# Cross-attention and a routed FFN on one core: another order of the attention's steps on four engines, and identity transposes in TensorE's waits

## The chip, the cores and the metric

The kernel runs on one core of a Trainium2 chip. Time is device time of one launch in microseconds (us). The kernel before took 2058.97 us, the median of three runs (2055.81 to 2060.05).

## The reference

Inputs: x (16 sequences of 224 tokens, 512 wide), a context (16 x 750 x 384) and a mask over the context. All arithmetic is in fp32.

```python
x = x + xattn(layernorm(x), ctx, mask, Wq, Wk, Wv, Wo, bo)    # 8 heads of 64, softmax over 750 keys
x = x + ffn(layernorm(x), Wr, W1, W2)                         # 8 experts, top 2, at most 1120 tokens each
# ffn: probs = softmax(xf @ Wr); for each expert e the tokens that chose it:
#      y[idx] += gate * (relu(xe @ W1[e]) @ W2[e])            # W1 512x2048, W2 2048x512
```

In the given inputs the unmasked keys that matter (see below) lie in the last 192 of the 750.

## The kernel before

**Arithmetic.** TensorE gets each fp32 operand as a high part and a low part (the remainder), and a product is three matrix products: high by high, high by low, low by high. ScalarE writes the high part while it copies a result out of PSUM, VectorE subtracts to get the low part. So a product that feeds another one is followed by a step on ScalarE and one on VectorE.

**Preamble** (`preamble`, L69). Identity, constants, a flag from the mask. Where every sequence has its masked-in keys only in the last 192 positions, the short attention runs (`attention_short`, L281), which is the case here.

**Attention.** The 16 sequences go in 8 pairs p. Each of a pair's steps has a kind and a number, and each engine executes its own steps in an order that is written out by hand in a string; a step waits on semaphores for what it needs, and everything behind it on its engine waits with it. On TensorE the kinds are:

- fc0-2, fx0-3: transposes of the context and of the normalized x of the *next* pair (written ahead for it); k0-3, q0-3, v0-3: projections; k0 and q0 too are those of the next pair.
- s0-15: scores of one head and sequence (16 units per pair), 192 keys. VectorE adds the mask and takes the maximum, ScalarE the exponential and its sum (2 instructions each), GpSimd the reciprocal and the scaling (u). Then t0-15: transposes of the probabilities (ScalarE and VectorE split them), then o0-15: the product with v (two heads share a result; the odd one ends it).
- A negative number (t-3, o-4) is a unit of the pair before: t13 to t15 and o12 to o15 of a pair are done in the pass after it. So are wo0-3 (output projection, residual, statistics of the second layernorm), tt0-3 (transposes of its result), lg0 (router logits) and lt0 (their transposes).

The kinds q, k, v, fx, fc, wo, tt, lg (`RINGED`) take turns in two PSUM banks psJ, in TensorE's order: each waits until the one two before it has been split or copied (`proj`, L731: `pe.wait_ge(proj_done, at - 1)`). Scores have psS0 and psS1, transposes psT, outputs psO.

Before the first pass a prologue (`PRO_ORDER`) does fc0 fc1 fc2 fx0 fx1 fx2 fx3 k0 q0 for pair 0, with the splits of the weights as they arrive. Pass 1 (p = 0) has the orders `*_FIRST`; passes 2 to 7 (p = 1 to 6) are a hardware loop with the orders `*_STEPS`; pass 8 is the same without what belongs to a next pair; the drain has `*_END`: the last units, wo, tt, lg, lt of pair 7. There are such strings for TensorE (PE), ScalarE (ACT), VectorE (DVE) and GpSimd (POOL).

**Router** (`router`, L1182). VectorE selects the top two of eight logits for each token (L1137 to L1144), counts them, and TensorE adds the counts (L1282) and computes the place of each token in its expert (`positions`, L1174). Meanwhile the first weight pairs of expert 0 load. The block ends for all engines together.

**Experts** (`experts`, L1408). VectorE turns places into tile and row (`place`, L1643), for expert 0 first; `early_slots` makes onehot matrices in 8 groups which TensorE multiplies with the token numbers (`early_product`, L1766), the result is copied (L1585) and GpSimd gathers rows by it (L1487). TensorE transposes them (`turn`, L1728), ScalarE and VectorE split them, and then 24 blocks of 3 tiles run: `hidden` (W1) and `output` (W2), 16 of each, through 1436 us. Ahead of the first hidden product's low half VectorE also clears three banks, splits eight weight pieces (L1129) and computes the gates (`gates`, L1149).

Of the kernel before, what the change touches and what calls it, by code (L numbers as in the profile page):

```python
# [16 lines left out]
F32 = mybir.dt.float32  # L17
# [11 lines left out]
E, F = 8, 2048  # L29
# [15 lines left out]
BLK = 3  # L45
# [124 lines left out]
def order(text):  # L170

    named = []
    for word in text.split():
        kind = word.rstrip("-0123456789")
        named.append((kind, int(word[len(kind):])))
    return named
# [18 lines left out]
    s0 t-3 o-4 q1 s1 k1 t-2 fs0 fs1 t-1 o-3 v0 o-2 fs2 fs3 q2 o-1 s2 wo0 fa0 wo1 t0 s3 o0 v1  # L195
    s4 wo2 fp0 ap0 ap1 t1 v2 s5 v3 tt0 ap2 o1 t2 fp1 tt1 o2 fp2 s6 t3 wo3 t4 s7 k2 fp3 o3
    s8 ap3 o4 q3 t5 k3 s9 fc0 tt2 t6 tt3 s10 fx0 s11 t7 s12 fx1 o5 o6 lg0 t8 lt0 fx2 t9
    s13 fc1 fc2 t10 o7 fx3 s14 o8 s15 t11 o9 k0 mb0 o10 q0 t12 o11
# [4 lines left out]
    u0 fl0 u1 tl0 tl1 u2 u3 tl2 u4 u5 u6 tl3 u7 u8 u9 u10 u11 bi0 bi1 u12 u13 u14 bi2 bi3 u15  # L203
# [77 lines left out]
def attention_short(nc, T, A):  # L281

    with ExitStack() as ctx:
# [29 lines left out]
        idle = x2T[:].rearrange("p c r -> p (c r)")  # L313
# [400 lines left out]
        def _(pe):  # L714
# [64 lines left out]
            def iteration(p, prev, nxt):  # L779
                for kind, i in pe_steps(prev, nxt):  # L780
# [43 lines left out]
                    elif kind in RINGED:  # L824
                        proj(p, prev, nxt, kind, i, p + 2)
                    elif kind == "lt":
                        out = bank(p, prev, nxt, "lg", 0)
                        held(pe, passed, lg_copied, p)
                        for t in range(TP):
                            mm = nc.tensor.transpose(out[0:R, TP * R + t * E:TP * R + (t + 1) * E], lgT[:, t * R:(t + 1) * R], ident[0:E, 0:E])  # L830
                        mm.then_inc(lg_t, 1)

            for kind, i in PRO_ORDER:
                if kind == "q":
                    pe.wait_ge(zeros, 6)
                proj(None, False, True, kind, i, 1)
            iteration(0, False, True)
# [344 lines left out]
def router(nc, T, A):  # L1182

    with ExitStack() as ctx:
# [14 lines left out]
        ps = ctx.enter_context(nc.psum_tensor("count_ps", [128, 512], F32))  # L1199
# [208 lines left out]
def experts(nc, T, A):  # L1408

    with ExitStack() as ctx:  # L1410
# [133 lines left out]
        def _(dve):  # L1544
# [31 lines left out]
            def early_slots():  # L1576
# [105 lines left out]
            then_gate(nc.vector.memset(T["vals"][:, :, :, 3], 1.0))  # L1682
            for n in range(NBLOCKS):
# [26 lines left out]
        def _(pe):  # L1710
# [216 lines left out]
```

## Time and profile before

| | us |
|---|---|
| median of 3 runs | 2058.97 |
| the profiled execution | 2061.44 |
| its span, first to last instruction | 2059.7 |
| TensorE busy in the span | 1954.4 |
| VectorE, ScalarE, GpSimd busy | 1002.4, 719.4, 477.0 |

The span has four parts: the prologue to 36 us, the attention's passes to 545, drain and router to about 590, and the experts. A view by stretches gives for each engine the busy time in a stretch of time, then the mean clock granted to TensorE as a share of 2.4 GHz (0.50 is 1.2 GHz). TensorE's instructions overlap in its pipeline, so that the start of the next one, not the length shown, tells the pace. In a timeline row the brackets hold how long the engine stood idle before it, and what ended that.

### The profile page before, as it was taken

How to read it: one execution, taken by the hardware profiler on the slowest of the kernel's cores; microseconds unless marked ns; L12 is line 12 of the kernel's file. 1: busy time of each engine (PE TensorE's matmuls, PEld its weight loads, DVE VectorE, ACT ScalarE, POOL GpSimd, SP SyncE). 2: the span in 40 equal slices, each digit the busy share in tenths (PEclk: the TensorE clock that was granted, in tenths of full speed). 3: DMA queues.
4: the chain of work that ended last, by engine and by line, in shares of the span. 5: the costliest groups of instructions: out<-in, count | busy, mean ns of one | idle time of the engine just before them, and what ended most of it. 6: DMA issues, size and time to landing. Idle time of an engine off the chain costs nothing.

```text
span 2059.7 us, 30182 instructions
## 1 busy us (share of the span) xinstructions
PE 1954.4 (95%) x11419; PEld 1733.6 (84%) x11419; DVE 1002.4 (49%) x2471; ACT 719.4 (35%) x1928; POOL 477.0 (23%) x560
## 2 busy tenths in 40 slices
PE   5799999999849999999999999999999999999997
PEld 4688888888638889989889888888998988889996
DVE  4678888887676353334133413432343353236221
ACT  4566776666414132123112311321132132115111
POOL 2445555455510021011001100111101011112101
PEclk9899999999959999999999999999999999999999
DMA  7011332211144144124112411341142144116102
GB/s 210 19 52 53 87 87 74 66 53 36 54 142 144 16 118 123 15 52 145 45 15 57 139 46 16 105 120 31 28 141 73 16 112 113 31 21 162 32 5 27
DMA packets 96316, 148.40 MB, mean 72 GB/s; under 512 B 8608, under 2 KB 50096, under 8 KB 96160
## 3 DMA queue, kind: packets, MB, share of 16 engines
q1 hardware_dynamic: 80288, 109.41, 16.9%
q0 software_dynamic: 15872, 36.71, 9.9%
q8 instruction: 123, 2.02, 0.4%
q14 instruction: 33, 0.27, 0.0%
HBM read 110.70 MB, written 35.39 MB: 71 GB/s over the span
## 4 chain that ended last, share of the span: by engine, by line
PE 69%; DVE 1%; issue 1%; POOL 0%; POOLq 0%; ACT 0%; DVEq 0%
PE psH L1714 33%; PE psY L1714 31%; PE psY L1753 2%; PE psX L1728 1%; PE psI L1776 1%; DVE w_lo L1129 0%; PE psI L1766 0%; POOL out_dram L1498 0%; POOLq L1410 0%; DVE hT_lo L1688 0%; PE psI L1782 0%; DVE moves L1564 0%; DVE onehot L1572 0%; DVE slot_tile L1649 0%; DVE ys L1647 0%
## 5 line engine op out<-in xcount | busy, mean ns | idle before, releaser
L1688 DVE SCALAR_TENSOR_TENSOR hT_lo<-psH,hT_hi 128x384 fp32r<-128x384 f32 (+1 forms) x384 | 210.0, 547 | 867.3 <-ACT hT_hi L1528 527.9
L1528 ACT ACTIVATE hT_hi<-psH 128x384 fp32r<-128x384 f32 (+1 forms) x384 | 185.4, 483 | 1063.3 <-PE psH L1714 1063.3
L1714 PE MATMUL psH<-xgT_hi,w_hi 128*128 128x256 f32 (+3 forms) x1536 | 477.7, 311 | 9.6 <-issue 8.8
L1714 PE MATMUL psH<-xgT_hi,w_lo 128*128 128x256 f32 (+3 forms) x1536 | 476.6, 310 | 2.1 <-issue 2.1
L1714 PE MATMUL psH<-xgT_lo,w_hi 128*128 128x256 f32 (+3 forms) x1536 | 475.3, 309 | 1.7 <-issue 1.7
L1714 PE MATMUL psY<-w_hi,hT_hi 128*128 128x512 f32 (+1 forms) x921 | 371.7, 404 | 0.0
L1714 PE MATMUL psY<-w_lo,hT_hi 128*128 128x512 f32 (+1 forms) x921 | 362.7, 394 | 1.1 <-issue 1.1
L1714 PE MATMUL psY<-w_hi,hT_lo 128*128 128x512 f32 (+1 forms) x921 | 362.3, 393 | 0.0
L1714 PEld LDWEIGHTS psH<-xgT_hi,w_hi 128*128 128x128 f32 x1536 | 291.5, 190 | 35.3 <-issue 18.5
L1714 PEld LDWEIGHTS psH<-xgT_lo,w_hi 128*128 128x128 f32 x1536 | 291.7, 190 | 14.9
L1714 PEld LDWEIGHTS psH<-xgT_hi,w_lo 128*128 128x128 f32 x1536 | 291.4, 190 | 4.1 <-issue 4.1
L1487 POOL DMA_INDIRECT xg<-xn_rows,gid x72 | 71.5, 993 | 854.8 <-PE psX L1728 455.6
L1714 PEld LDWEIGHTS psY<-w_hi,hT_lo 128*128 128x128 f32 (+1 forms) x921 | 171.5, 186 | 41.1
L1498 POOL DMA_INDIRECT out_dram<-ys,sid x72 | 113.6, 1578 | 394.8 <-DVE ys L1620 380.2
L1714 PEld LDWEIGHTS psY<-w_lo,hT_hi 128*128 128x128 f32 (+1 forms) x921 | 172.5, 187 | 27.1 <-issue 1.4
L1714 PEld LDWEIGHTS psY<-w_hi,hT_hi 128*128 128x128 f32 (+1 forms) x921 | 172.2, 187 | 24.4 <-DVE hT_lo L1688 0.2
L1129 DVE TENSOR_TENSOR w_lo<-stage,w_hi 128x512 fp32r<-128x512 f32 x256 | 164.9, 687 | 2.6 <-ACT w_hi L1124 2.6
L1124 ACT ACTIVATE w_hi<-stage 128x512 fp32r<-128x512 f32 x256 | 146.6, 626 | 29.1 <-DMA stage<-in_L_ffn_W_dram 28.9
L469 POOL TENSOR_TENSOR rsum<-ssum,minus_one 112x2 f32<-112x2 f32 x128 | 91.1, 712 | 187.8 <-ACT probs L537 187.8
L537 ACT ACTIVATE probs<-probs,nmax 112x192 f32<-112x192 f32 x256 | 113.9, 450 | 41.8 <-DVE nmax L648 41.5
L471 POOL TENSOR_TENSOR probs<-probs,rsum 112x384 f32<-112x384 f32 x128 | 108.7, 849 | 10.0
L648 DVE CUSTOM_DVE_ANT_0 probs<-psS,mask_bias 112x192 f32<-112x192 f32 x256 | 80.0, 352 | 15.4 <-PE psS L793 14.5
(229 smaller groups left out, 2870.2 us busy)
## 6 DMA issues: line engine op xcount, KB each, us to landing
stage<-in_L_ffn_W_dram SPq DMA_DIRECT2D x128, 512.0 KB, 4.5
x_sb<-in_x_dram SPq DMA_DIRECT2D x8, 896.0 KB, 5.6
x_res<-in_x_dram SPq DMA_DIRECT2D x8, 896.0 KB, 5.6
out_dram<-x_res SPq DMA_DIRECT2D x8, 896.0 KB, 4.8
xn_rows<-xn SPq DMA_DIRECT2D x8, 896.0 KB, 4.8
c_sb<-in_ctx_dram SPq DMA_DIRECT2D x8, 384.0 KB, 6.2
c_sb<-in_ctx_dram SPq DMA_DIRECT2D x32, 96.0 KB, 5.8
out_dram<-zrow SPq DMA_DIRECT2D x9, 256.0 KB, 4.2
```

Source lines behind the costliest of these rows:

```text
L469: nc.gpsimd.tensor_tensor(rsum[:, i % 4, :], ssum[:, i % 4, :], T["minus_one"][0:R, :], ALU.pow).then_inc(recip, 1)
L471: nc.gpsimd.tensor_tensor(probs(i), probs(i), rsum[:, i % 4, :].unsqueeze(2).to_broadcast([R, 2, NKEY]), ALU.mult).then_inc(normed, 1)
L537: e = nc.scalar.activation(probs(i)[:, it, :], probs(i)[:, it, :], ACT.Exp, bias=nmax[:, i % 4, it:it + 1], scale=-1.0, accum_out=ssum[:, ...
L648: s = nc.vector.tensor_tensor_reduce(out=probs(i)[:, it, :], in0=psS[i % 2][0:R, it * NKEY:(it + 1) * NKEY], in1=mb[:, b, mask_order(half( ...
L1124: nc.scalar.activation(piece(T, 0, pair, j), staged(T, pair, j), ACT.Copy).then_inc(T["w_hi_done"], 1)
L1129: engine.tensor_tensor(piece(T, 1, pair, j), staged(T, pair, j), f32(piece(T, 0, pair, j)), ALU.subtract).then_inc(T["w_lo_done"], 1)
L1487: nc.gpsimd.indirect_dma_start(out=xg[0:m, t, :], out_offset=None, in_=A["xn2"], in_offset=bass.IndirectOffsetOnAxis(ap=gid[e % 2][0:m, c: ...
L1498: nc.gpsimd.indirect_dma_start(out=A["out"], out_offset=bass.IndirectOffsetOnAxis(ap=sid[e % 2][0:m, c:c + 1].bitcast(U32), axis=0), in_=y ...
L1528: h = nc.scalar.activation(hT[0][:, f % 2, 0:m], psH[f % 2][:, 0:m], ACT.Relu)
L1688: h = nc.vector.scalar_tensor_tensor(out=hT[1][:, f % 2, 0:m], in0=psH[f % 2][:, 0:m], scalar=0.0, in1=f32(hT[0][:, f % 2, 0:m]), op0=ALU. ...
L1714: mm = nc.tensor.matmul(out, stationary(a, c), moving(b, c), start=first and c == chunks[0] and j == 0, stop=last and c == chunks[-1] and ...
L1753: mm = nc.tensor.matmul(psY[t][0:2 * PART, :], hP[:, f % 2, :], w2[b][:, f, :], start=f == 0 and b == 0, stop=f == FCH - 1 and b == 1, ski ...
```

## The change

1. New orders for the steps on all four engines, in the loop, in the first pass and in the drain. The steps are the same ones; only their order changes.
2. A helper `turn_over` transposes the identity matrix a given number of times into a PSUM bank that nothing else uses at that time, with no wait of its own and nobody waiting for it. It stands in the prologue (the numbers are in `IDLE`, one for each step that it goes ahead of, and 16 at the end), in the drain (x6, x10, x4, x5), in the router (32 at the start, 8 at the end) and at the start of the experts (16, 48, and 4 behind each of four transposes).
3. At the start of the experts, `place` for experts 1 to 7 moves behind the gates, and the clearing of two banks moves into `early_slots`, ahead of VectorE's wait for the last early product.

```diff
--- before.py
+++ after.py
@@ -60,6 +60,12 @@
         engine.wait_ge(sem, value)
 
 
+def turn_over(nc, T, bank, times):
+
+    for _ in range(times):
+        nc.tensor.transpose(bank[:, 0:128], T["ident"][:], T["ident"][:])
+
+
 def held(engine, passed, sem, value):
 
     engine.wait_ge(sem, value)
@@ -178,51 +184,56 @@
 
 
 PE_STEPS = order("""
-    t-3 q1 s0 k1 o-4 t-2 o-3 s1 s2 t-1 v0 s3 q2 o-2 o-1 t0 wo0 wo1 s4 v1 wo2 t1 v2 o0 v3 s5 o1 tt0 t2 t3
-    s6 s7 tt1 wo3 o2 t4 k2 o3 q3 t5 s8 k3 o4 t6 s9 s10 fc0 o5 tt2 t7 s11 tt3 fx0 o6 fx1 t8
-    s12 lg0 o7 fx2 t9 lt0 s13 o8 fc1 t10 fc2 o9 t11 s14 fx3 s15 k0 q0 o10 o11 t12
+    q1 t-3 o-4 s0 k1 o-3 t-2 s1 s2 t-1 v0 s3 q2 o-2 t0 wo0 o-1 s4 v1 wo1 v2 t1 o0 s5 v3 wo2 t2 tt0 o1 s6 t3 tt1 s7 o2
+    wo3 t4 o3 k2 q3 s8 t5 s9 k3 o4 fx0 t6 s10 o5 tt2 t7 fx1 o6 tt3 s11 t8 s12 fc0 lg0 o7 fx2 t9 lt0 s13 o8 fc1 t10 fc2
+    s14 o9 t11 s15 fx3 o10 t12 k0 q0 o11
 """)
 
 
...
 
 
 PE_FIRST = order("""
-    s0 s1 q1 s2 k1 v0 s3 t0 v1 s4 t1 o0 v2 s5 t2 o1 v3 q2 s6 t3 o2 k2 s7 t4 o3 q3 s8 t5 o4 k3
-    s9 t6 fc0 o5 s10 t7 fc1 o6 fx0 s11 t8 o7 fc2 fx1 s12 t9 o8 fx2 s13 t10 o9 fx3 s14 t11 o10 k0 s15 t12 q0 o11
+    s0 v1 k1 s1 s2 q1 s3 v0 t0 v2 t1 s4 v3 o0 s5 t2 s6 o1 t3 k2 o2 s7 t4 o3 q2 q3 k3 t5 s8 o4 t6 fc0 s9 s10 o5 o6 t7 fc1
+    s11 t8 o7 s12 t9 o8 s13 fx0 t10 o9 fx1 fc2 s14 fx2 t11 fx3 o10 k0 q0 t12 s15 o11
 """)
 ACT_FIRST = order("""
-    s0 s1 q1 s2 k1 v0 t0 s3 v1 t1 s4 o0 w10 v2 t2 s5 o1 w11 v3 q2 t3 s6 o2 w12 k2 t4 s7 o3 w13 q3 t5 s8 o4 k3
-    t6 s9 fc0 o5 t7 s10 fc1 o6 fx0 t8 s11 o7 fc2 fx1 t9 s12 o8 fx2 t10 s13 o9 fx3 t11 s14 o10 k0 t12 s15 q0 o11
+    v1 k1 s0 s1 q1 w10 s2 v0 w11 s3 t0 o0 v2 w12 t1 v3 t2 s4 t3 k2 o1 s5 o2 t4 s6 o3 q2 q3 s7 t5 t6 k3 o4 w13 o5 s8 t7
+    fc0 s9 t8 s10 fc1 o6 t9 o7 fx0 s11 t10 fx1 fc2 fx2 fx3 t11 s12 o8 k0 o9 s13 q0 t12 o10 s14 s15 o11
 """)
...
-POOL_FIRST = order("u0 u1 u2 u3 u4 u5 fl0 u6 u7 u8 u9 u10 u11 bi0 u12 bi1 u13 bi2 u14 bi3 u15")
-
-
-PE_END = order("t-3 o-4 t-2 o-3 wo0 t-1 o-2 wo1 o-1 wo2 tt0 wo3 tt1 tt2 tt3 lg0 lt0")
-ACT_END = order("t-3 o-4 t-2 o-3 t-1 o-2 o-1")
-DVE_END = order("t-3 o-4 t-2 o-3 wo0 t-1 o-2 wo1 o-1 ap0 wo2 ap1 tt0 wo3 ap2 tt1 ap3 tt2 tt3 lg0 lt0")
+POOL_FIRST = order("""
+    u0 u1 u2 u3 u4 u5 u6 fl0 u7 bi0 u8 u9 u10 bi1 u11 u12 u13 u14 u15 bi2 bi3
+""")
+
+
+PE_END = order("o-4 t-3 t-2 o-3 o-2 t-1 wo0 o-1 wo1 x6 wo2 tt0 wo3 x10 tt1 x4 tt2 tt3 x5 lg0 lt0")
+IDLE = {("fc", 0): 22, ("fc", 2): 4, ("fx", 0): 7, ("fx", 2): 4, ("k", 0): 2, ("q", 0): 3}
+ACT_END = order("""
+    t-3 t-2 o-4 o-3 o-2 t-1 o-1
+""")
+DVE_END = order("""
+    t-3 t-2 o-4 o-3 t-1 wo0 o-2 o-1 wo1 ap0 wo2 tt0 ap1 ap2 wo3 tt1 tt2 ap3 tt3 lg0 lt0
+""")
 
 
 RINGED = ("q", "k", "v", "fx", "fc", "wo", "tt", "lg")
@@ -823,6 +834,8 @@
                             mm.then_inc(o_mm, 1)
                     elif kind in RINGED:
                         proj(p, prev, nxt, kind, i, p + 2)
+                    elif kind == "x":
+                        turn_over(nc, T, psS[1], i)
                     elif kind == "lt":
                         out = bank(p, prev, nxt, "lg", 0)
                         held(pe, passed, lg_copied, p)
@@ -833,7 +846,9 @@
             for kind, i in PRO_ORDER:
                 if kind == "q":
                     pe.wait_ge(zeros, 6)
+                turn_over(nc, T, psS[1], IDLE.get((kind, i), 0))
                 proj(None, False, True, kind, i, 1)
+            turn_over(nc, T, psS[1], 16)
             iteration(0, False, True)
             pe.wait_ge(T["b_in"], 32)
             with pe.Fori(1, NPAIR - 1) as p:
@@ -1196,7 +1211,7 @@
         steps_i, steps, signs = sb("steps_i", [R, LEVELS], I32), sb("steps", [R, LEVELS]), sb("signs", [R, NBLK, LEVELS])
         over_step, signed = sb("over_step", [R, E, LEVELS]), sb("signed", [R, NBLK, E, LEVELS])
         extra = sb("extra", [R, NBLK, E])
-        ps = ctx.enter_context(nc.psum_tensor("count_ps", [128, 512], F32))
+        ps, idle = [ctx.enter_context(nc.psum_tensor(n, [128, 512], F32)) for n in ("count_ps", "idle_ps")]
         iotas, consts, step, counted, counts = sem("iotas"), sem("consts"), sem("step"), sem("counted"), sem("counts")
         marks, placed, tables = sem("marks"), sem("placed"), sem("tables")
         block = ctx.enter_context(nc.Block())
@@ -1277,10 +1292,12 @@
 
         @block.tensor
         def _(pe):
+            turn_over(nc, T, idle, 32)
             pe.wait_ge(consts, 5)
             pe.wait_ge(counts, 1)
             nc.tensor.matmul(ps[0:R, 0:E], T["ones_m"][:], cnt[:], start=True, stop=True).then_inc(counted, 1)
             positions(pe, nc, T, marks, placed)
+            turn_over(nc, T, idle, 8)
             pe.wait_ge(placed, 1)
 
 
@@ -1581,6 +1598,8 @@
                                         ALU.mult).then_inc(early_done, 1)
                 for q in range(GROUPS):
                     slot_onehot(0, 0, q)
+                for bank in psH:
+                    nc.vector.memset(bank[:], 0.0)
                 dve.wait_ge(slot_mm, GROUPS)
                 nc.vector.tensor_copy(gid[0][:], psI[:, 0:CAPT]).then_inc(ids_ready, 1)
 
@@ -1657,10 +1676,7 @@
             then(nc.vector.scalar_tensor_tensor(out=T["slot_tile"][:], in0=pos, scalar=1.0, in1=T["keep"][:], op0=ALU.add, op1=ALU.mult))
             place(slice(0, 1))
             early_slots()
-            place(slice(1, E))
-            for bank in (*psH, psY[BLK - 1]):
-                s = nc.vector.memset(bank[:], 0.0)
-            s.then_inc(cleared, 1)
+            nc.vector.memset(psY[BLK - 1][:], 0.0).then_inc(cleared, 1)
             for pair in range(EARLY):
                 for j in range(PIECES):
                     split_pair_lo(nc.vector, T, 0, pair, j)
@@ -1680,6 +1696,7 @@
             nc.vector.tensor_copy(T["vals"][:, :, :, 1], f32(T["gate_hi"]))
             nc.vector.tensor_tensor(T["vals"][:, :, :, 2], T["gate"], f32(T["gate_hi"]), ALU.subtract)
             then_gate(nc.vector.memset(T["vals"][:, :, :, 3], 1.0))
+            place(slice(1, E))
             for n in range(NBLOCKS):
                 e, k = divmod(n, NBLK)
                 for f in range(FCH):
@@ -1806,10 +1823,13 @@
                 return nc.values_load(T["more"][0:1, n:n + 1], engines=(mybir.EngineType.PE,), min_val=0,
                                       max_val=1, skip_runtime_bounds_check_because="it is a comparison's result")
 
+            turn_over(nc, T, psY[0], 16)
             for q in range(GROUPS):
                 early_product(q)
+            turn_over(nc, T, psY[0], 48)
             for c in range(DCH):
                 turn(0, c)
+                turn_over(nc, T, psY[0], 4)
             pe.wait_ge(cleared, 1)
             hidden(0, 0, True)
             full = more(0)
```

## Rows read from the trace of the kernel before

**Rows 1.** The page: TensorE's busy time, and its granted clock in 40 slices.
```profile
PE 1954.4 (95%) x11419; PEld 1733.6 (84%) x11419; DVE 1002.4 (49%) x2471; ACT 719.4 (35%) x1928; POOL 477.0 (23%) x560
...
PEclk9899999999959999999999999999999999999999
```

**Rows 2.** Stretches: start:end, length, busy by engine, clock, DMA share, GB/s.
```profile
36.00:105.00 69.00, 54.60 (x305) 49.13 (x306) 39.69 (x127) 39.05 (x121) 29.68 (x36) 0.81 0.25 70
105.00:171.80 66.80, 63.40 (x407) 55.12 (x406) 53.66 (x165) 43.03 (x132) 31.54 (x45) 0.97 0.22 61
171.80:234.80 63.00, 61.90 (x410) 53.90 (x410) 52.66 (x159) 42.44 (x132) 33.95 (x47) 1.00 0.25 72
...
486.70:545.00 58.30, 55.37 (x363) 47.44 (x361) 41.89 (x135) 37.20 (x120) 31.37 (x43) 1.00 0.16 48
545.00:577.00 32.00, 23.90 (x107) 14.60 (x105) 13.79 (x28) 3.52 (x11) 9.18 (x15) 0.89 0.18 58
577.00:623.00 46.00, 20.38 (x79) 17.86 (x79) 36.11 (x93) 9.01 (x18) 8.53 (x31) 0.52 0.38 125
623.00:2059.00 1436.00, 1412.59 (x8077) 1268.20 (x8075) 534.40 (x1087) 361.58 (x848) 191.01 (x146) 1.00 0.27 70
```

**Rows 3.** TensorE's waits in pass 1, 36 to 105 us.
```profile
PE psO L721 <- DVE pT_lo L655: 4.7, 5, 1.9
PE psO L721 <- DVE vb_lo L590: 3.7, 1, 3.7
```

**Rows 4.** TensorE's waits in five passes of the loop, 171.8 to 486.7 us.
```profile
PE psO L721 <- DVE vb_lo L590: 3.6, 5, 0.7
PE psJ L772 <- DVE k L590: 1.9, 5, 0.4
```

**Rows 5.** TensorE's timeline in the prologue: start, length, instruction.
```profile
12.16 1.97 PE L748 MATMUL psJ<-ident,c_sb 128*128 128x128 f32 x8 [8.32 <-issue]
...
31.44 0.57 PE L721 MATMUL psJ<-xT_lo,w_hi 128*128 128x448 f32 x1
31.82 0.53 PE L721 MATMUL psJ<-xT_hi,w_lo 128*128 128x448 f32 x1
35.99 0.50 PE L793 MATMUL psS<-k,q_hi 128*112 128x192 f32 x1 [3.64 <-DVE q_lo L590]
```

**Rows 6.** TensorE's timeline at full clock.
```profile
63.12 0.36 PE L721 MATMUL psJ<-xT_lo,w_hi 128*128 128x448 f32 x1
63.32 0.36 PE L721 MATMUL psJ<-xT_hi,w_lo 128*128 128x448 f32 x1
...
226.47 0.60 PE L748 MATMUL psJ<-ident,c_sb 128*128 128x128 f32 x4
226.91 0.26 PE L802 MATMUL psT<-ident,probs 112*128 112x112 f32 x1
...
283.56 3.17 PE L776 MATMUL psJ<-x2T,wr 128*8 128x448 f32 x8
```

**Rows 7.** TensorE's timeline in the drain.
```profile
558.31 0.45 PE L721 MATMUL psJ<-w_hi,oT_hi 128*112 128x512 f32 x1 [1.54 <-DVE oT_lo L660]
...
567.50 0.57 PE L772 MATMUL psJ<-ident,xn 112*128 112x112 f32 x4 [1.98 <-DVE xn L632]
...
570.55 5.31 PE L776 MATMUL psJ<-x2T,wr 128*8 128x448 f32 x8 [0.81 <-DVE x2T L678]
```

**Rows 8.** Timeline from the router to the first output product, TensorE and VectorE.
```profile
585.03 0.51 PE L1282 MATMUL count_ps<-cnt,ones_m 112*112 112x8 f32 x2 [8.02 <-DVE cnt L1246]
...
594.22 7.27 PE L1766 MATMUL psI<-early_ids,onehot 112*128 112x10 f32 x32 [5.85 <-DVE onehot L1572]
...
608.64 1.43 PE L1728 MATMUL psX<-ident,xg 128*128 128x128 f32 x6 [7.15 <-DMA xg<-xn_rows,gid]
...
619.45 0.53 DVE L1688 SCALAR_TENSOR_TENSOR hT_lo<-psH,hT_hi 128x352 fp32r<-128x352 f32 x1
...
621.91 0.63 PE L1714 MATMUL psY<-w_hi,hT_hi 128*128 128x512 f32 x1
```

More of the change, by code:

```diff
@@ L184 @@
+    s14 o9 t11 s15 fx3 o10 t12 k0 q0 o11
 """)
 ACT_STEPS = order("""
-    o-4 t-3 q1 k1 t-2 o-3 s0 v0 t-1 o-2 q2 o-1 s1 t0 s2 v1 s3 o0 v2 t1 v3 o1 t2 s4 s5 t3 s6 o2 t4 k2 o3
-    s7 q3 t5 k3 s8 o4 fc0 t6 o5 t7 s9 fx0 fx1 t8 s10 s11 fx2 t9 o6 s12 fc1 fc2 o7 t10 t11 fx3 o8 o9
-    s13 k0 o10 s14 q0 o11 t12 s15
+    t-3 o-4 q1 k1 t-2 s0 o-3 o-2 s1 v0 t-1 q2 s2 o-1 t0 v1 v2 t1 s3 s4 v3 t2 t3 s5 o0 o1 s6 s7 o2 o3 t4 k2 q3 t5 o4 k3
+    fx0 t6 s8 s9 fx1 t7 s10 t8 o5 o6 s11 fc0 s12 o7 fx2 t9 fc1 fc2 t10 s13 t11 o8 fx3 o9 t12 s14 k0 q0 s15 o10 o11
@@ L191 @@
 """)
 DVE_STEPS = order("""
[L195 to L198, printed above, removed]
+    o-4 t-3 s0 q1 k1 s1 fs0 fs1 t-2 o-3 v0 fs2 s2 t-1 fs3 q2 wo0 o-2 o-1 s3 fa0 s4 v1 t0 wo1 fp0 v2 s5 fp1 ap0 ap1 v3 t1
+    o0 wo2 t2 tt0 fp2 tt1 t3 s6 s7 ap2 wo3 o1 t4 fp3 k2 o2 o3 ap3 s8 s9 q3 t5 k3 o4 fx0 t6 tt2 s10 fx1 tt3 s11 o5 s12 t7
@@ L199 @@
+    fc0 t8 lg0 lt0 fx2 t9 o6 s13 fc1 o7 t10 fc2 s14 fx3 o8 t11 k0 s15 t12 o9 q0 mb0 o10 o11
 """)
 POOL_STEPS = order("""
-    u0 fl0 u1 tl0 tl1 u2 u3 tl2 u4 u5 u6 tl3 u7 u8 u9 u10 u11 bi0 bi1 u12 u13 u14 bi2 bi3 u15
+    u0 u1 tl0 u2 fl0 tl1 u3 u4 tl2 u5 u6 tl3 u7 u8 u9 u10 u11 bi0 u12 u13 u14 u15 bi1 bi2 bi3
 """)
 PE_FIRST = order("""
-    s0 s1 q1 s2 k1 v0 s3 t0 v1 s4 t1 o0 v2 s5 t2 o1 v3 q2 s6 t3 o2 k2 s7 t4 o3 q3 s8 t5 o4 k3
-    s9 t6 fc0 o5 s10 t7 fc1 o6 fx0 s11 t8 o7 fc2 fx1 s12 t9 o8 fx2 s13 t10 o9 fx3 s14 t11 o10 k0 s15 t12 q0 o11
+    s0 v1 k1 s1 s2 q1 s3 v0 t0 v2 t1 s4 v3 o0 s5 t2 s6 o1 t3 k2 o2 s7 t4 o3 q2 q3 k3 t5 s8 o4 t6 fc0 s9 s10 o5 o6 t7 fc1
@@ L214 @@
 """)
 DVE_FIRST = order("""
-    s0 s1 q1 s2 k1 v0 s3 t0 v1 s4 t1 o0 w10 v2 fs0 fs1 s5 t2 o1 w11 v3 fs2 fs3 q2 fa0 s6 t3 o2 w12 k2 s7 t4 o3 w13 q3
-    fp0 fp1 s8 t5 o4 k3 fp2 fp3 s9 t6 fc0 o5 s10 t7 fc1 o6 fx0 s11 t8 o7 fc2 fx1 s12 t9 o8 fx2 s13 t10 o9 fx3 s14 t11 o10 k0
-    s15 t12 mb0 q0 o11
-""")
-POOL_FIRST = order("u0 u1 u2 u3 u4 u5 fl0 u6 u7 u8 u9 u10 u11 bi0 u12 bi1 u13 bi2 u14 bi3 u15")
-PE_END = order("t-3 o-4 t-2 o-3 wo0 t-1 o-2 wo1 o-1 wo2 tt0 wo3 tt1 tt2 tt3 lg0 lt0")
-ACT_END = order("t-3 o-4 t-2 o-3 t-1 o-2 o-1")
@@ L225 @@
-DVE_END = order("t-3 o-4 t-2 o-3 wo0 t-1 o-2 wo1 o-1 ap0 wo2 ap1 tt0 wo3 ap2 tt1 ap3 tt2 tt3 lg0 lt0")
+    s0 v1 s1 s2 k1 s3 q1 w10 v0 s4 t0 w11 o0 v2 t1 s5 v3 t2 t3 s6 w12 fs0 k2 fs1 o1 o2 fs2 t4 fs3 q2 o3 s7 fa0 q3 s8 fp0
+    t5 o4 s9 t6 k3 o5 fp1 t7 s10 fp2 fp3 o6 t8 s11 fc0 t9 fc1 fx0 o7 s12 fx1 fc2 t10 fx2 fx3 o8 w13 s13 t11 k0 s14 s15
+    o9 o10 t12 q0 mb0 o11
+""")
+POOL_FIRST = order("""
+    u0 u1 u2 u3 u4 u5 u6 fl0 u7 bi0 u8 u9 u10 bi1 u11 u12 u13 u14 u15 bi2 bi3
+""")
+PE_END = order("o-4 t-3 t-2 o-3 o-2 t-1 wo0 o-1 wo1 x6 wo2 tt0 wo3 x10 tt1 x4 tt2 tt3 x5 lg0 lt0")
```

## The prediction

> **What bounds the kernel now.** I read the page's busy shares and clock line first, then the stretches, then TensorE's waits in each stretch, then its timeline where it stood still. TensorE is busy in 95% of the span and the clock line shows dips at the start, in the slices around 570 to 620 us and one late [rows 1]. The stretches [rows 2] say where a change to the attention can earn. Pass 1 of the attention (pair 0, 36 to 105 us) holds TensorE for 69.0 us, of which it is busy 54.6 at a mean granted clock of 0.81. Pass 2 takes 66.8. A pass of the loop takes 63.0 with TensorE busy 61.9 at clock 1.00; five such rows are alike to 0.1 us, one stands. Then come the last pass (58.3), the drain of the last pair's rows (32.0, busy 23.9, clock 0.89), the router and the start of the experts (46.0, busy 20.4, clock 0.52), and 1436 us of experts with TensorE full at clock 1.00, which the change leaves alone. So the loop is TensorE-bound with 1.1 us of standing time a pass, whatever order its steps have; pass 1, the drain and the router stretch are bound by chains through all engines and run in part at 1.2 GHz instead of 2.4.
>
> **Part by part.** All sums are made on the profiled execution: 2061.44 us around a span of 2059.7. The median of the three runs is 2058.97, 2.5 us lower; I carry that over unchanged.
>
> *a. Turns ahead of pass 1.* What one turn of the identity costs: eight 128x128 transposes at the start take 1.97 us, less the last one's own length of about 0.5 that is 1.47 / 7 = 0.21 us each at the low clock [rows 5]; four in the loop are followed by the next instruction after 0.44 us, 0.11 each at the full one [rows 6]. The 22 before fc0 cost at most 4.7 us and lie in a wait of 8.3 us for the context load; the 4, 7, 4, 2 and 3 further on cost at most 0.8, 1.5, 0.8, 0.4 and 0.6 us, in waits for VectorE of about that size; the 16 after q0 cost at most 3.4 us in the wait of 3.64 before s0 [rows 5]. So even cold they delay nothing by more than some tenths. What they may bring is the clock: the products of q0 start 0.38 us apart [rows 5] where the same ones later start 0.20 apart [rows 6], so 12 of them cost 12 x 0.18 = 2.1 us more than at the full clock. k0 ahead of it is cold too, but q0 waits for weights split on VectorE, not for k0. Value -2.0; bounds 0 (still cold) and -3 (the transposes' chain gets shorter as well).
>
> *b. Pass 1.* Its work at full clock is about 54.6 x 0.81 = 44 us; 69.0 - 54.6 = 14.4 us are waits, and 54.6 - 44 = 10 us are what the low clock costs. The greatest waits are those before an output product (4.7 us in five for pT_lo and 3.7 in one for vb_lo) and the 3.6 before s0 [rows 3]. I count the work between steps with a product of n columns at n/448 of 0.20 us [rows 6]. In the old order v1 and v2 come late, and t0, t1 and t6 to t10 stand only 1.2 to 2.0 us of work ahead of their o. The new one brings v1 straight after s0, puts o1 behind v3, t2 and s6, t0 and t1 3.7 us ahead of their o, and s0 to s7 6.5 to 11 us ahead of their t. It also makes tighter places: q1 to v2, q2 to k3 and q3 to fc0 (every second projection shares a bank, and the split of a q took 3.64 us after its last product [rows 5], but only 2.4 to 2.7 us of work lie between them), and t7 to t9 stand 0.9 to 1.3 us ahead of their o, no better than before. I add these up to 6 us, and take 8 us of waits for the pass. Low clock followed waits of 2 to 4 us; with those filled I leave 2 us for it. 44 + 8 + 2 = 54, against 69: -15. Bounds: -25 (nothing but the 44) and -5 (the waits only change places). VectorE's and ScalarE's own work in the pass, 39.7 and 39.1 us [rows 2], puts no higher floor.
>
> *c. Pass 2.* It costs 66.8 - 63.0 = 3.8 us more than a later one: TensorE waits for q0's split, which ScalarE does behind s15, and then runs cold for a while. In the new orders ScalarE takes q0 ahead of s14 and s15. Value -3.5, bounds 0 and -4.
>
> *d. The loop.* The same 77 steps on TensorE. Two waits recur in each pass, 3.6 us in five before an output product and 1.9 in five before tt2 [rows 4], 0.7 and 0.4 us. The first goes, since o1 now stands behind wo2, t2 and tt0. The second moves: fx0 comes after q3 s8 t5 s9 k3 o4, 2.9 us of work where q3's split wants 3.6, so it waits 0.7, and tt2 then finds k3 ready. Net -0.4 us a pass, with the last pass six: -2.5. Bounds: all 1.1 us go in each (-7), or two new waits of 0.7 us come (+8).
>
> *e. The drain.* 32.0 - 23.9 = 8.1 us of waits, and the router product takes 5.31 us [rows 7] where it takes 3.17 in the loop [rows 6], 2.1 us of clock. New order: t15 and o14 go ahead of wo0, and o15 ahead of wo1, so wo1's 2.8 us cover o15's split and the 1.54 us before wo2 go [rows 7]; x6, x10, x4, x5 fill waits (x10 costs 1.1 to 2.1 us in a wait of 1.98 [rows 7]). The wait after wo3 for statistics, root and scaling stays: it is the last chain. -1.5 (o15) -2.1 (clock) and -1.4 of the waits ahead of wo0: -5. Bounds -7 and -1.
>
> *f. Router.* VectorE's chain of selections sets it, and nothing on it changes. 32 turns cost 3.5 to 6.8 us in a wait of 8.02 [rows 8]. The 8 behind the position product stand in front of the end of the block for all engines; cold they are 1.7 us, of which VectorE's last tables cover some; I take half. Value +0.5, bounds 0 and +1.2.
>
> *g. Start of the experts.* 16 turns (1.8 to 3.4 us) lie in a wait of 5.85, 48 in one of 7.15 [rows 8]. At full clock 48 cost 5.3 and are hidden; at the low one 10.2 and run 3 us over the gathered rows. Tiles 1 to 7 are placed 3 us of VectorE later, after the gates, and two of three memsets go into a wait; but all of it still lies before VectorE's first hT_lo, which ends at 619.98 and with the warm product before it releases the output product at 621.91 [rows 8]. VectorE's queue there gets shorter by the memsets and by what the early product gains (7.27 us at the low clock, but paced in part by VectorE's comparisons, so I take 1 of them), about 2 us together; the output product itself, cold in the row, gives 0.5 more. Value -2.5; bounds -4.5 and +5 (turns cold).
>
> Sum: -2.0 - 15 - 3.5 - 2.5 - 5 + 0.5 - 2.5 = -30.0, so 2031.4 us for the profiled execution and 2029 on the scale of the median.
>
> A rule that speaks against a, e and g. The trace shows that transposes run twice as fast when the full clock is granted, 0.11 against 0.21 us [rows 5, 6]; whether they bring it about it leaves open, though 28 of them between 12 and 23 us did not keep q0 from running cold. The Trainium skill, TensorE: Matmul & The Clock Gate (Part 4: PE-mode transpose) says that the full clock does not engage for transposes, because they do not count as a busy array in the same way. By the page a turn is filler that costs and gives nothing; rival 1 works that out from rows.
>
> **Rivals.**
> 1. *Turns do not hold the clock.* Then a gives 0, e only -3, the 48 turns at 0.21 us delay the first gathered rows by 3 us and the sixteen between the first transposes add 1.5 more, so g is +4 and f +1; b keeps its better order but not all of the clock, -11; c -2, d -2.5. Sum -13.5: 2045.5. For it speaks the cold q0 behind 28 transposes; against it, that those stood with gaps between them.
> 2. *Everything falls into place.* Pass 1 near its 44 us (-23), the loop at -7, the drain -6, the rest as forecast: -43.5 or 2015. For it speaks that TensorE's work in the loop already runs with 1.1 us of waits; against it the three tight bank places in b.
> 3. *The loop's new order costs more than the front gains (slower).* One mechanism: steps of VectorE and ScalarE stand in fixed order, and one step put ahead of what it waits for holds all behind it. In pass 1 such a place cost 3.65 us before o1. In the loop it is paid six times and again in the last pass; two of them per pass are 7 x 7.3 = 51 us, less 30 gained elsewhere: 2080. It decides from 30 / 7 = 4.3 us a pass. Against it: the tightest places in the new order are short by 0.7 us, and VectorE has 63.0 - 52.7 = 10 us of room a pass [rows 2].
> 4. *The orders do not help.* Waits in pass 1 only change places and the loop loses 1 us a pass: about -2, no change.
>
> **How the numbers follow.** Forecast 0.58, rival 1 0.20, rival 2 0.12, rival 3 0.07, rival 4 0.03. 0.2% (4 us) is what a measurement of this kernel can tell. Faster by more: 0.90, within: 0.03, slower: 0.07. The time is the likeliest case's, 2029. The range reaches down past rival 2 with room for its own bounds, to 2011, and up past rival 1, to 2053; what lies outside is rivals 3 and 4 and a tail of the others.
>
> **What would show it.** The span from s0 to the first t13 is 54 us rather than 69; q0's products start 0.20 us apart; the loop's passes take 62.6 us, with a wait before fx0 and none before o1; the router product in the drain takes 3.2 us; TensorE's clock is 1.00 from the first products of the attention to the router, and the 48 turns end before the gathered rows land. The forecast is wrong if a pass of the loop is longer than 64 us, if pass 1 stays above 60, or if the turns start 0.21 us apart throughout.

## The result, and the profile after

| | before | after | forecast |
|---|---|---|---|
| median, us | 2057.39 (4 runs) | 2044.52 (4 runs, 2041.94 to 2045.82) | 2029, range 2011 to 2053 |
| ratio after to before | | 0.9924 (0.9899 to 0.9949) | |
| profiled execution | 2061.44, span 2059.7 | 2044.1, span 2042.4 | |

The change saves 12.9 us, 0.8%. The time lies in the range and on the side forecast, but the gain is less than half of the 30 us that I had. That it comes within 1 us of what rival 1 was given (2045.5) is chance: its mechanism is not what happened. The parts below are read from the profiled executions, whose spans differ by 17.3 us, since that of before was 4 us above its median. Medians are of fast runs; of all runs here one was in the slow state, a fourth one of the last experiment (e11) with 2744.55 us at a mean granted clock of 0.65 (the others: 0.97 to 0.99).

Two lines of the page, to be laid beside [rows 1]:

```profile
PE 1966.6 (96%) x11622; PEld 1749.8 (86%) x11622; DVE 1000.8 (49%) x2471; ACT 715.5 (35%) x1928; POOL 477.4 (23%) x560
...
PEclk9999999999889999999999999999999999999999
```

The clock line of before has its dips in the second and the twelfth slice; a late one, of which the forecast speaks, is not in it.

The stretches of after, with borders at the same steps as in [rows 2] (start:end, length, busy by engine, clock, DMA share, GB/s):

```profile
34.60:85.40 50.80, 45.72 (x304) 41.74 (x305) 39.56 (x128) 38.73 (x118) 25.25 (x32) 0.97 0.36 102
85.40:147.50 62.10, 61.73 (x411) 53.61 (x411) 53.20 (x164) 42.46 (x136) 34.82 (x48) 1.00 0.25 70
147.50:209.40 61.90, 61.53 (x411) 53.60 (x410) 52.30 (x160) 42.00 (x132) 33.98 (x46) 1.00 0.26 73
456.90:512.70 55.80, 55.01 (x362) 47.09 (x360) 43.00 (x141) 37.54 (x122) 30.90 (x42) 1.00 0.17 51
512.70:540.20 27.50, 23.25 (x130) 16.64 (x129) 13.97 (x29) 3.25 (x10) 10.00 (x15) 1.00 0.20 67
540.20:590.80 50.60, 34.26 (x194) 31.42 (x194) 34.13 (x89) 9.50 (x19) 9.52 (x31) 0.74 0.36 114
590.80:2042.40 1451.60, 1420.82 (x8079) 1275.38 (x8079) 536.09 (x1091) 360.47 (x847) 190.52 (x146) 0.99 0.27 69
```

The last two lines end and begin with the first hT_lo of the experts; before, the experts from that point on took this (same view):

```profile
619.50:2059.70 1440.20, 1416.09 (x8091) 1271.50 (x8090) 536.43 (x1090) 362.60 (x850) 191.01 (x146) 0.99 0.27 69
```

So the attention with its drain gained 36.9 us (its last step starts at 539.75, before at 576.65), more than forecast. Then 19.7 us were lost again: the way from there to the first hT_lo takes 51.1 us, before 42.8, and the experts from there on 1451.6, before 1440.2, although nothing in them was changed. I had -2.0 for the first and 0 for the second.

**The attention.** TensorE's waits in pass 1, and in five passes of the loop (engine and line, what it waited for: us in total, times, longest):

```profile
PE psJ L732 <- DVE q_lo L601: 2.1, 2, 1.1
PE psS L804 <- DVE q_lo L601: 1.9, 1, 1.9
PE psT L813 <- POOL probs L482: 1.4, 2, 0.8
PE psO L732 <- DVE pT_lo L666: 1.0, 2, 0.6
```
```profile
PE psJ L755 <- DVE q_lo L601: 1.8, 5, 0.4
```

The waits of [rows 3] before output products are gone but for 1.0 us; pass 1 stands idle for 5.1 us in place of 14.4. In the loop one wait of 0.4 us before fx0 is left, where the forecast had put it with 0.7. TensorE's timeline in the prologue and in the drain:

```profile
11.21 4.29 PE L66 MATMUL psS<-ident 128*128 128x128 f32 x22 [7.22 <-issue]
15.33 1.04 PE L759 MATMUL psJ<-ident,c_sb 128*128 128x128 f32 x8
...
30.38 0.37 PE L732 MATMUL psJ<-xT_lo,w_hi 128*128 128x448 f32 x1
30.58 0.36 PE L732 MATMUL psJ<-xT_hi,w_lo 128*128 128x448 f32 x1
30.79 1.91 PE L66 MATMUL psS<-ident 128*128 128x128 f32 x16
34.58 0.34 PE L804 MATMUL psS<-k,q_hi 128*112 128x192 f32 x1 [1.89 <-DVE q_lo L601]
```
```profile
530.68 1.26 PE L66 MATMUL psS<-ident 128*128 128x128 f32 x10
...
535.79 3.17 PE L787 MATMUL psJ<-x2T,wr 128*8 128x448 f32 x8 [0.26 <-DVE x2T L689]
...
539.75 0.35 PE L843 MATMUL psJ<-ident,lgT 8*112 8x8 f32 x4 [0.80 <-DVE lgT L693]
```

q0's products start 0.20 us apart instead of 0.38, and the router product takes 3.17 us instead of 5.31. But the wait of 8.3 us ahead of the first transpose in [rows 5] gives the turns no room: they need only the identity, which is ready at 1.6 us, and still start at 11.21, behind 7.22 us that the profile puts down to nothing. They run after this wait and not in it, and the context's transposes move from 12.16 to 15.33.

**From the drain to the experts.** Timeline of after, TensorE, VectorE, GpSimd and the DMA issues of SyncE (SPq):

```profile
551.29 1.92 PE L66 MATMUL idle_ps<-ident 128*128 128x128 f32 x8
...
554.42 0.43 DVE L1676 SCALAR_TENSOR_TENSOR slot_tile<-psI,xg 112x256 f32<-112x256 f32 x1 [2.45 <-PEq L1199]
...
564.65 6.89 PE L66 MATMUL psY<-ident 128*128 128x128 f32 x48
564.83 0.17 DVE L1604 CAST gid<-psI 128x9 int32<-128x9 f32 x1
565.30 1.97 POOL L1504 DMA_INDIRECT xg<-xn_rows,gid  x1 [21.96 <-DVE gid L1604]
568.00 0.37 SPq L1131 DMA_DIRECT2D stage<-in_L_ffn_W_dram  x1
...
576.26 0.85 PE L1745 MATMUL psX<-ident,xg 128*128 128x128 f32 x3 [4.72 <-DMA xg<-xn_rows,gid]
...
587.77 0.39 DVE L1666 SCALAR_TENSOR_TENSOR ys<-slot_tile,skip 112x224 f32<-112x224 f32 x1
...
590.84 0.52 DVE L1705 SCALAR_TENSOR_TENSOR hT_lo<-psH,hT_hi 128x352 fp32r<-128x352 f32 x1
```

The same in before:

```profile
601.53 0.17 DVE L1585 CAST gid<-psI 128x9 int32<-128x9 f32 x1 [1.11 <-PE psI L1766]
...
608.80 0.37 SPq L1116 DMA_DIRECT2D stage<-in_L_ffn_W_dram  x1
```

From row numbers (gid) to the first transpose of gathered rows it is 11.4 us; before it was 608.64 - 601.53 = 7.1. The turns are not the cause, TensorE then stands idle for 4.72 us. The weight loads from 568.0 on fit: before, the first of them was issued at 608.8, when the rows had landed. And from the first transpose to the first hT_lo it is 14.6 us, before 10.8, with `place` (587.77 to 590.81) directly ahead of hT_lo. Behind its 4.72 us of standing TensorE also runs these transposes and the turns between them at the low clock (0.50 in 577 to 580).

**In the experts.** TensorE's waits that no releaser ends (from 623 us on), two of the three longest, and the 10 us around each:

```profile
PE psH L1731 <- issue: 17.6, 15, 3.9
```
```profile
708.59 0.58 PE L1731 MATMUL psH<-xgT_hi,w_lo 128*128 128x256 f32 x1 [2.52 <-issue]
...
763.32 0.37 PE L1731 MATMUL psH<-xgT_lo,w_hi 128*128 128x256 f32 x1 [3.85 <-issue]
```
```profile
705.00:715.00 10.00, 6.93 (x29) 6.12 (x29) 2.62 (x4) 0.49 (x1) 4.79 (x4) 0.66 0.52 69
760.00:770.00 10.00, 6.68 (x28) 6.06 (x28) 3.94 (x7) 1.67 (x4) 4.84 (x3) 0.66 0.82 142
```

They stand at the borders of blocks, and the clock falls behind them. Before, these waits came to 10.3 us in all, the longest 2.1. Another 2.0 us of the 11.4 is a wait of TensorE for VectorE's hT_lo right at the start of the stretch (591.4), which before does not have. The page counts 125 transfers on the instruction queue with 2.05 MB, 16.4 KB each.

### The profile page after: what moved, and what is told of

It is laid out like the page before. It is cut to its first block, busy times and chain, and to the rows that moved or that the text cites. A ratio compares the mean times of both kernels' runs of the same rounds, so it can differ in the third digit from the quotient of the medians.

```text
span 2042.4 us, 30593 instructions
## 1 busy us (share of the span) xinstructions
PE 1966.6 (96%) x11622; PEld 1749.8 (86%) x11622; DVE 1000.8 (49%) x2471; ACT 715.5 (35%) x1928; POOL 477.4 (23%) x560
## 3 DMA queue, kind: packets, MB, share of 16 engines
q8 instruction: 125, 2.05, 0.4%
## 4 chain that ended last, share of the span: by engine, by line
PE 70%; issue 1%; DVE 1%; DMA 0%; POOL 0%; POOLq 0%; ACT 0%; DVEq 0%
PE psH L1731 33%; PE psY L1731 32%; PE psY L1770 2%; PE psX L1745 2%; PE psI L1793 1%; DMA xg<-xn_rows,gid 0%; DVE onehot L1589 0%; POOL xg L1504 0%; PE psI L1783 0%; POOL out_dram L1515 0%; PE psY L66 0%; DVE w_lo L1144 0%; POOLq L1427 0%; DVE hT_lo L1705 0%; PE psI L1799 0%
## 5 line engine op out<-in xcount | busy, mean ns | idle before, releaser
L548 ACT ACTIVATE probs<-probs,nmax 112x192 f32<-112x192 f32 x256 | 113.4, 447 | 11.5 <-DVE nmax L659 11.4
```

What stands on the lines that cost most here:

```text
L548: e = nc.scalar.activation(probs(i)[:, it, :], probs(i)[:, it, :], ACT.Exp, bias=nmax[:, i % 4, it:it + 1], scale=-1.0, accum_out=ssum[:, ...
```

## The experiments

Theory after the traces: the attention's new order works; `place` and the weight loads it lets through cost 8 us at the experts' start; and the 203 turns, two instructions each, push the experts' code to a place where it is fetched at worse moments. Rivals: the turns' own time, and chance in the transfers. Times are medians; the ratio is to runs of before on the same chip. Positions are set by transposes in the body of `threshold`, which is never executed here but lies ahead of the experts in TensorE's program.

### No turns

```diff
- turn_over(...) at all places, x6 x10 x4 x5 out of PE_END     # 203 turns
+ 203 transposes in threshold, not executed
```

> The kernel after without any of the 203 turns; orders and the moved place stay; 203 turns that are never executed stand in a branch ahead of the experts, so that the experts' instructions keep their position. The trace of after shows the attention 36.9 us shorter than before. If turns hold the clock, their absence shows in the attention: clock below 0.9 in the drain and in parts of pass 1, drain end 3 to 6 us later than after's 540.1 us. If the orders alone do the work, the drain ends within 2 us of 540. In the experts' start the turns can only cost: without the 8 in the router and the four groups of 4 the way from the drain's end to the first hT_lo should be 1 to 2 us shorter. Turns matter: 2046 to 2051. Turns are filler: 2041 to 2044.

2044.91 us against 2059.4, ratio 0.9925 (0.9911 to 0.9940): as after, between the two expectations, and no difference that can be measured. The trace shows both halves. The drain's last step starts at 542.7 us, after's at 539.8, so the turns bring 2.9 us; in the first hT_lo 1.4 of them are left (592.3 against 590.8). The turns neither make nor break the attention's 37 us. In the prologue the context's transposes start at 11.1 us without turns (15.3 in after), q0's products at 27.2 (28.2), 0.37 us apart, and s0 at 35.5 (34.6).

### Before, with the experts' code shifted

```diff
 # before.py
+ 203 transposes in threshold, not executed
```

> The kernel before, with 203 identity transposes (406 instructions) in the threshold branch, which is never executed: only the position of the experts' instructions in TensorE's program changes, by as much as in the kernel after. After loses 11 to 12 us in the experts, of it 7 in waits that nothing explains at block borders and the rest in low clock behind them. If instruction fetch at shifted positions makes these waits: 2066 to 2070 us, with waits of 2 to 4 us near the ends of the first blocks. If they come from how the data transfers fall: 2057, as before.

2072.2 us against 2059.4, ratio 1.0058 (1.0039 to 1.0076): the first theory, 2 us beyond its range. Nothing that is executed differs. TensorE's waits without releaser are like those in after, and the two greatest sit at the same borders:

```profile
PE psH L1716 <- issue: 17.2, 16, 3.3
```
```profile
737.32 0.39 PE L1716 MATMUL psH<-xgT_hi,w_lo 128*128 128x256 f32 x1 [2.83 <-issue]
...
790.75 0.37 PE L1716 MATMUL psH<-xgT_lo,w_hi 128*128 128x256 f32 x1 [3.31 <-issue]
```
```profile
619.20:2070.60 1451.40, 1421.28 (x8090) 1275.10 (x8089) 536.63 (x1090) 362.27 (x850) 190.36 (x146) 0.99 0.27 69
```

The experts take 1451.4 us, 11 us more than in before. The position of the code costs it, not the way up to there, which takes 619.2 us as in before (619.5).

### After, with the code back in place modulo 16 KB

```diff
 # after.py
+ 53 transposes in threshold, not executed    # 203 + 53 = 256
```

> The kernel after, with 53 more identity transposes in the same branch that is never executed: 203 + 53 = 256 pairs of instructions, so positions are those of the kernel before plus 512. Fetches in the trace carry 16 KB, 256 instructions of 64 bytes. If the position within such a piece decides: the experts take the 1376 us (first to last block) of before again, 2033 us in all. If not: 2044, and experts at 1387.

2036.19 us, ratio 0.9885 (0.9871 to 0.9900): 8.3 us under after, for code that never runs, and 3 above the 2033 expected.

```profile
PE psH L1733 <- issue: 11.8, 15, 2.3
```
```profile
592.50:2035.00 1442.50, 1416.19 (x8079) 1270.56 (x8079) 536.29 (x1091) 360.63 (x846) 190.93 (x146) 0.99 0.28 69
```

To the span's end (2035.4) the experts take 1442.9 us, 2.7 more than in before; 2.6 of them is the wait for VectorE's hT_lo at their start, which after has too.

### place back where it was

```diff
             early_slots()
+            place(slice(1, E))
...
             then_gate(nc.vector.memset(T["vals"][:, :, :, 3], 1.0))
-            place(slice(1, E))
```

> The kernel after, with place for experts 1 to 7 back behind early_slots, ahead of the weight splits. Theory: moved behind the gates it lies on VectorE's chain to the first hT_lo (3.1 us), and the weight splits, now earlier, release transfers of 2 MB that meet the gather (row numbers ready to first transpose 11.4 us against 7.1 before). So 5 to 7 us shorter: 2038. Rival: the way to the first hT_lo is set by the sum of VectorE's work and only the gather changes, 0 to 2 us; or the gather is late because of the turns in front of it and nothing changes, 2044.

2039.06 us, ratio 0.9906 (0.9891 to 0.9920): 5.5 under after. Row numbers at 565.3, first transpose at 573.0, first hT_lo at 582.3: 7.7 and 9.3 us where after has 11.4 and 14.6, so 9.1 us less on this way. The experts stay at the bad position (1453.8 us), 2.2 more than in after.

### The turns on the old orders

```diff
 # before.py, with turns as in after and x6 x10 x4 x5 in the old PE_END;
 # the clearing of two banks as in after, place where it was
+ 53 transposes in threshold, not executed
```

> The kernel before with the 203 turns where the kernel after has them (old orders, place where it was, two of the three memsets ahead of the last early product), and 53 more turns in the branch that is never executed, so that the experts sit as in before. Theory that turns buy little: the old pass 1 waits in places that no turn fills, its dips in the clock stay, only s0 comes 1 us earlier and the drain 1 to 2: 2054 to 2057. Theory that the clock was the loss: pass 1 sheds 5 us and the drain 3, 2046 to 2050.

2057.24 us against 2060.76, ratio 0.9987 (0.9972 to 1.0003): the smaller theory. The trace has s0 at 34.4 (before 36.0), the drain's last step at 572.0 (576.65), loop passes at 63.0 us.

### All that helped

```diff
 # after.py
   place as above
-  turn_over(nc, T, idle, 8)
+ 61 transposes in threshold, not executed    # 256 in all
```

> The kernel after with place back behind early_slots, without the 8 turns behind the position product, and with 61 turns in the branch that is never executed (256 in all). If the two gains of the first experiments are independent (-8.3 from the position, -5.5 from place) and the router's end gives 1 more: 2029 to 2031. If they share a cause, for instance transfers that meet fetches: 2035.

2025.2 us against 2060.76, ratio 0.9840 (0.9812 to 0.9867). Better than both kernels, by 1.6% and by 0.8%. It lies below both expectations and below the sum of the parts (0.9862 by their ratios), which its interval still holds. Row numbers, the weight load behind the gathers, and the first transpose:

```profile
563.94 0.17 DVE L1605 CAST gid<-psI 128x9 int32<-128x9 f32 x1
...
570.13 0.37 SPq L1131 DMA_DIRECT2D stage<-in_L_ffn_W_dram  x1
...
571.82 0.52 PE L1746 MATMUL psX<-ident,xg 128*128 128x128 f32 x3 [0.43 <-DMA xg<-xn_rows,gid]
572.18 0.60 PE L66 MATMUL psY<-ident 128*128 128x128 f32 x4
```

### The same without turns

```diff
 # e6
- all turns; 256 transposes in threshold, not executed
```

> As e6, but no turn is executed; 256 stand in the branch. In the first experiment the turns gained 2.9 us up to the drain's end and lost half of it again by the first hT_lo. Turns worth what the attention shows: 2032 to 2034, 2 to 3 us over e6. Turns worth nothing: the same as e6 within 1 us.

2029.09 us, ratio 0.9860 (0.9833 to 0.9886). 3.9 us by the medians, with intervals that overlap; the traces' first hT_lo lies at 586.9 against 581.1. Where nothing else holds up the start, the turns seem worth about 4 us, more than the 2 to 3 expected.

### Half a piece further

```diff
 # e6
+ 64 more transposes in threshold, not executed    # 320 in all
```

> As e6, but with 64 more turns in the branch, 128 instructions, half a fetched piece. If the position within 16 KB decides, the waits at block borders sit elsewhere and are others in length: the experts' time moves by 3 to 12 us in either direction from 1378. If only the total shift of after was unlucky: the same as e6.

2033.3 us, ratio 0.9876 (0.9851 to 0.9901), 8.1 over e6. Up to the first hT_lo at 581.1 the two traces are alike to 0.1 us; from there 1450.5 us against 1439.4.

### Only the first pass's orders; only the loop's

```diff
 # before.py with PE_FIRST, ACT_FIRST, DVE_FIRST, POOL_FIRST of after   (e9)
 # before.py with PE_STEPS, ACT_STEPS, DVE_STEPS, POOL_STEPS of after   (e10)
```

> The kernel before with the new orders of the first pass alone (four engines), no turns, position unchanged. The trace of after has pass 1 at 50.8 us against 68.9 and pass 2 at 62.1 against 66.9. If the order of pass 1 does this by itself and also hands the loop its first pass in better state: 2059 - 18 - 4 = 2037. If the gain needs the new loop orders behind it or the turns: 2042 to 2046.

2037.82 us against 2058.57, ratio 0.9904 (0.9882 to 0.9926): the first theory. Four strings for one pass of eight bring 20.7 us, with old loop orders and no turns. The mean granted clock of pass 1 is 0.97, as in after.

The prologue, which this edit leaves alone, comes out otherwise than in before:

```profile
28.44 0.36 PE L723 MATMUL psJ<-xT_lo,w_hi 128*128 128x448 f32 x1
28.64 0.36 PE L723 MATMUL psJ<-xT_hi,w_lo 128*128 128x448 f32 x1
...
33.24 0.50 PE L795 MATMUL psS<-k,q_hi 128*112 128x192 f32 x1 [3.63 <-DVE q_lo L592]
```

Without a turn q0's products start 0.20 us apart, and s0 starts 2.7 us earlier than in before, 1.3 earlier than in after. The same holds in e10 (s0 at 33.6), but not in the two other kernels without turns whose prologue is the same, e1 (35.5) and e7 (35.8), nor in e2 (35.75).

> The kernel before with the new orders of the loop alone (passes 2 to 8), no turns, position unchanged. Read from the traces, a pass takes 61.9 instead of 63.0 us: 7 passes x 1.1 = 8 us, 2051. My forecast had 0.4 a pass, 2056.

2050.21 us, ratio 0.9955 (0.9941 to 0.9969): 8.4 us, as read from the traces and not as forecast; passes of 61.9 us.

### place behind the first hT_lo

```diff
 # e6, without place behind early_slots
                     h.then_inc(h_lo, 1)
+                    if n == 0 and f == 0:
+                        place(slice(1, E))
```

> As e6, but place for experts 1 to 7 stands behind VectorE's first hT_lo: off its chain, but with the weight splits still right behind the early slots, as in after. If the loss in after was the 3.1 us of place in the chain: as e6 or 1 us better, 2024 to 2025, and the first transpose 7 to 8 us after the row numbers. If the weight transfers that start early hold up the gather: first transpose 10 to 11.5 us after the row numbers, and 2027 to 2029.

2031.55 us, the middle of three runs (2027.44 to 2032.85), ratio 0.9860 (0.9836 to 0.9883) to 2058.57, which makes 2029.8: the second theory, and rather more than it had.

```profile
563.20 0.17 DVE L1605 CAST gid<-psI 128x9 int32<-128x9 f32 x1
...
566.37 0.37 SPq L1131 DMA_DIRECT2D stage<-in_L_ffn_W_dram  x1
...
574.90 0.85 PE L1747 MATMUL psX<-ident,xg 128*128 128x128 f32 x3 [4.52 <-DMA xg<-xn_rows,gid]
575.54 1.06 PE L66 MATMUL psY<-ident 128*128 128x128 f32 x4
```

The first transpose comes 11.7 us after the row numbers, about as in after, and 7.9 in e6. So the costs of the moved `place` are apart. The late gather costs 3.8 us itself and then 2.3 more: TensorE has stood for 4.5 us, and its transposes and turns run at the low clock (1.06 us for four turns, 0.60 in e6), so that the first hT_lo comes 11.6 us after the first transpose instead of 9.3. `place` costs its own length on VectorE's chain, 3.0 us (14.6 in after).

Why the gather is late is shown in part. The weight loads go out 3.2 us after the row numbers instead of 6.2, while GpSimd still issues the gathers. GpSimd's own time is not it: the gather instruction during which VectorE's weight splits begin takes longer, the first in e11 (1.97 us against 1.24 in e6) and the third in e6 (1.89 against 0.94), but in both kernels the third ends 5.2 us after the row numbers. From there to the first transpose it is 6.5 us here and 2.7 in e6. No run moved the weight loads without the splits that release them.

## Why the prediction was right in direction and wrong in size

| step | forecast | measured | |
|---|---|---|---|
| a. turns ahead of pass 1 | -2.0 | -1.4 | full clock in q0, but q0 1.0 us later than in e1 |
| b. pass 1 | -15 | -18.2 | 5.1 us of waits where I had left 8 |
| c. pass 2 | -3.5 | -4.7 | |
| d. loop and pass 8 | -2.5 | -8.0 | 5 x -1.1 and -2.5 |
| e. drain | -5 | -4.6 | |
| f, g. router to first hT_lo | -2.0 | +8.3 | 1.0 by the 8 turns, -0.8 by faster early products, 4.3 to the first transpose, 3.8 behind it |
| experts after it | 0 | +11.4 | 2.0 waiting for the first hT_lo, the rest position of the code |

- *b, c, d.* The mechanism was right and the sizes too small. In d I had q3's split want the same 3.6 us in the loop as in the prologue; the wait before fx0 came out at 0.4 instead of 0.7, and pass 8 had waits of its own that I did not read. e9 and e10 show that orders alone do it: 20.7 and 8.4 us.
- *a, e.* The clock went as forecast where the turns stand. But it was a small part: the turns alone are worth 3.5 us on the old orders (e5, not clear of zero) and nothing measurable in after (e1). What had lowered the clock in pass 1 were the waits, and the orders removed these (0.97 in e9, without a turn). In *a* it was wrong that the turns delay nothing "by more than some tenths": with them the context's transposes start 4.2 us later than in e1 and q0 1.0 us. And the full clock in q0 is no proof of the turns, since e9 and e10 have it without any; that part of *a* came out right in part by luck.
- *g is the step that failed.* "all of it still lies before VectorE's first hT_lo" took VectorE's work as one sum. But the order in it mattered: ahead of the gather's landing VectorE had time free, behind it none. `place` lay in that free time and was moved to where each of its 3.0 us counts. And what it left behind started earlier, released the staging buffers and let SyncE send 2 MB of weights against the gather, which then came 4 us later and left TensorE cold. I had written down neither what the earlier splits would trigger nor that SyncE waits for them. The forecast was -2.5 for g; measured were 4.3 + 3.8 - 0.8 = +7.3. e4 and e11 show both costs.
- *f.* The 8 turns are cold and stand in front of the block's end: VectorE waits for TensorE 2.45 us there, before 1.45. I had 0.5. The early products, which run faster behind 16 turns, give 0.8 back: from VectorE's first step of the experts to the row numbers it is 10.4 us (554.42 to 564.83), before 11.2.
- *The experts.* No step spoke of the position of code, and "the change leaves alone" was wrong for this reason. The Trainium skill, Runtime: NRT & Kernel Launch (Instruction fetch mechanics) says that instructions are fetched in blocks of 16 KB, in sequence, and that a taken branch whose target is not there yet waits for its block. The runs agree as far as they show it: the page has 16.4 KB a transfer, the waits stand at block borders (one of two variants of a block is jumped over), a shift of 203 pairs costs 9 to 11 us in two kernels, one of 256 at most 3 (e3, e6), one of 320 costs 11 in the trace and 8 by the medians again (e8 against e6). Which fetch is late at which branch was not shown.

*Rival 1* held that turns do not hold the clock, after the Trainium skill, TensorE: Matmul & The Clock Gate (Part 4: PE-mode transpose). For these fp32 transposes the trace speaks against the page. In the prologue nothing but turns had run since 11.21, and the eight transposes at 15.33 take 1.04 us against 1.97 in [rows 5]. The 48 turns of after go from one level to the other while they run, 9 in 2.13 us and then 28 in 3.22 (TensorE's timeline, two stretches of one row):

```profile
565.13 2.13 PE L66 MATMUL psY<-ident 128*128 128x128 f32 x9
```
```profile
568.32 3.22 PE L66 MATMUL psY<-ident 128*128 128x128 f32 x28
```

*Rival 2* was nearer than the forecast for the attention with its drain (36.9 us; it had 41.5 there, I had 28.0), *rival 3* and *4* are out: passes of 61.9 us.

## What to carry to other kernels

When engines run fixed orders, look first at the pass that nothing precedes: four strings for one pass in eight gave 20.7 us, those for seven passes 8.4, and fillers for the clock almost nothing once the waits were gone. Before a piece of work is moved, ask whether it lies in a wait, and what starts earlier in its place: 3 us of vector work cost 9 us up to the first hT_lo and 5.5 by the medians (after against e4), most of it through a gather that came late and a TensorE gone cold behind it. Where a long unrolled program has branches, a change of its length upstream can move the time by 0.5% and more; put never-executed instructions ahead of it to tell that from the change itself, before you judge either.

## What the hardware showed unexpectedly

- Instructions that never run cost or gave 8 to 13 us: 2059.4 to 2072.2 (e2), 2044.5 to 2036.2 (e3), 2025.2 to 2033.3 (e8).
- Transposes of the identity bring TensorE to its full clock, 0.21 to 0.11 us each. But the same prologue without turns ran q0 at 0.37 us a product in before, e1, e2 and e7 and at 0.20 in e9 and e10.
- At the start of the attention TensorE stands 7 to 8 us, until 11.1 to 12.2 us, in every kernel. In e1 the profile puts this down to the context load, but identity transposes, which need none, start no earlier (11.2 in after, 11.3 in e5). That this is its code on the way was not tried.
- The gather instruction of GpSimd during which VectorE's weight splits begin takes 0.7 to 0.9 us longer: the first in after (1.97 us, before 1.24), the third in e6 (1.89, before 0.94).
